# Four node stages of a graph network: the normalized rows made by ScalarE instead of VectorE

## The reference: what is computed

```python
def _layernorm(x, axis=-1, eps=1e-05):
    m = jnp.mean(x, axis=axis, keepdims=True)
    v = jnp.var(x, axis=axis, keepdims=True)
    return (x - m) / jnp.sqrt(v + eps)
...
x = _layernorm(x + _L0_gnn_ref(x, edge_weight, src, dst, ...))
x = _layernorm(x + _L1_gnn_ref(x, L1_gnn_factors, src, dst, ...))
x = _layernorm(x + _L2_gnn_ref(x, edge_index, L2_gnn_W, L2_gnn_a_l, L2_gnn_a_r))
x = _layernorm(x + _L3_gnn_ref(x, L3_gnn_W_in, L3_gnn_W_out, src, dst))
```

## Time and profile before

| | |
|---|---|
| median of 3 runs | 5793.68 us (5790.52 to 5794.18) |
| the profiled execution: its own time | 5795.6 us |
| its span from first to last instruction | 5793.8 us |
| busy share of the span: PE, DVE, ACT, POOL | 59%, 42%, 24%, 63% |
| mean granted TensorE clock | 0.735 of full speed |

### The profile page before, as it was taken

How to read it: one execution, slowest core, us unless ns; L and a number is a source line. 1 busy time by engine, 2 the same in 40 slices (tenths; PEclk the granted TensorE clock), 3 DMA queues, 4 the chain that set the end, 5 groups by cost and what they waited for, 6 DMA issues and landing times. The chain is left out here.

```text
span 5793.8 us, 95902 instructions
## 1 busy us (share of the span) xinstructions
PE 3447.0 (59%) x19621; PEld 2711.1 (47%) x19621; DVE 2417.4 (42%) x3906; ACT 1387.4 (24%) x3059; POOL 3658.6 (63%) x3808
## 2 busy tenths in 40 slices
PE   1258988889669998466666662333333443333335
PEld 0246565556458886466656561333333333333333
DVE  3323333333546666366666664222222222222224
ACT  0012222222224443133333231111111211111111
POOL 2267777777611013777777774777777767777776
PEclk9779999999889999588888885555555565555557
DMA  9969999999479997466666653455544444444443
GB/s 231 306 183 291 298 300 301 304 298 296 124 234 332 327 331 231 138 182 181 181 181 186 177 168 87 131 131 131 131 131 131 124 114 131 131 131 131 131 131 106
DMA packets 809797, 1127.80 MB, mean 195 GB/s; under 512 B 128769, under 2 KB 490874, under 8 KB 806362
## 3 DMA queue, kind: packets, MB, share of 16 engines
q1 hardware_dynamic: 368424, 431.55, 24.3%
q0 software_dynamic: 134688, 305.12, 21.5%
q10 hardware_dynamic: 306588, 390.09, 20.2%
HBM read 688.68 MB, written 438.07 MB: 194 GB/s over the span
## 5 line engine op out<-in xcount | busy, mean ns | idle before, releaser
L1114 POOL DMA_INDIRECT gath<-sender_table,idx x1664 | 1570.2, 944 | 577.0 <-issue 413.5
L1318 DVE TENSOR_TENSOR_SCAN scan<-meta,scan,bank 128x512 f32<-128x512 bf16 x624 | 798.6, 1280 | 1943.2 <-DVEq L1315 1942.8
L1187 PE MATMUL bank<-ident,gath 128*128 128x128 f32 x1664 | 464.1, 434 | 1277.5 <-DMA gath<-sender_table,idx 1277.5
L1114 POOL DMA_INDIRECT gath<-joint_table,idx x832 | 810.4, 974 | 298.9 <-issue 208.2
L1507 POOL DMA_INDIRECT gath<-attention_table,idx x832 | 814.1, 978 | 263.3 <-issue 191.7
L1187 PEld LDWEIGHTS bank<-ident,gath 128*128 128x128 f32 x1664 | 297.8, 217 | 1443.5 <-DMA gath<-sender_table,idx 1443.5
L1255 ACT ACTIVATE rows<-bank 128x512 f32<-128x512 f32 x624 | 372.6, 597 | 1149.9 <-ACTq L1253 1121.5
L738 POOL DMA_INDIRECT gath<-scan_rows,end_i x196 | 188.9, 964 | 646.2 <-ACTq L1432 574.7
L1213 PE MATMUL bank<-ident,scan 128*128 128x128 f32 x2496 | 568.6, 373 | 4.5 <-PEq L1211 4.5
L1213 PEld LDWEIGHTS bank<-ident,scan 128*128 128x128 f32 x2496 | 470.6, 202 | 130.5 <-issue 130.5
L1194 PE MATMUL bank<-ident,gath 128*128 128x128 f32 x1664 | 372.5, 309 | 0.0
(11 more groups left out here) (239 smaller groups left out, 5569.5 us busy)
## 6 DMA issues: line engine op xcount, KB each, us to landing
recv<-receiver_rows SPq DMA_DIRECT2D x624, 256.0 KB
scan_rows<-rows ACTq DMA_DIRECT2D x624, 256.0 KB
attention_scan_rows<-rows ACTq DMA_DIRECT2D x208, 264.0 KB
receiver_rows<-gath ACTq DMA_DIRECT2D x26, 2048.0 KB, 12.1
meta<-edge_meta SPq DMA_DIRECT2D x208, 256.0 KB
factor_rows<-gath ACTq DMA_DIRECT2D x208, 256.0 KB
meta<-edge_meta SPq DMA_DIRECT2D x416, 128.0 KB
gath<-factor_rows SPq DMA_DIRECT2D x208, 256.0 KB
```

The source lines that it names most:

```text
L1114: pool.indirect_dma_start(out=landed[s][:, c, 0:width], out_offset=None, in_=table[:, :], in_offset=bass.IndirectOffsetOnAxis(ap=idx[s][:, ...
L1187: ins = pe.transpose(b[:, c * P:(c + 1) * P], g[:, c, 0:F], ident[:, :])
L1318: chain(v.tensor_tensor_scan(scan[s % 2][:, :], go_on, src, scan[1 - s % 2][:, EB - 1:EB], ALU.add if k == 1 else ALU.mult, ALU.max if k = ...
```

## The change

DVE no longer writes the normalized rows. Its piece `normalize` becomes `scale`, with two small instructions per group: the reciprocal of the deviation (as before) and shift = -mean x reciprocal. ACT gets a piece `normalize` of the same lag, placed behind `turned_x` and ahead of `deviation`: for each tile an ACTIVATE of the function Identity with the reciprocal as its scale and the shift as its bias, one number per partition each. `rstd` has two buffers now, and `shift` too. Three semaphores are new: `n_scale` (DVE to ACT, once per group), `n_scale_free` and `n_y_free` (ACT to DVE: the scale's and `y_nm`'s buffers may be written again, two groups later).

```diff
-        stats = sb("stats", [P, CT, 6]); mv = [sb(f"mv{s}", [P, CT, 2]) for s in range(2)]; std = [sb(f"std{s}", [P, CT]) for s in range(2)]; rstd = sb("rstd", [P, CT])
+        stats = sb("stats", [P, CT, 6]); mv = [sb(f"mv{s}", [P, CT, 2]) for s in range(2)]; std = [sb(f"std{s}", [P, CT]) for s in range(2)]; rstd = [sb(f"rstd{s}", [P, CT]) for s in range(2)]; shift = [sb(f"shift{s}", [P, CT]) for s in range(2)]
...
+        n_scale = sem("n_scale"); n_scale_free = sem("n_scale_free"); n_y_free = sem("n_y_free")
...
 def update(q, s):
...
+                    if norm and q > 0:
+                        v.wait_ge(n_y_free, 1)
+                        v.sem_inc(n_y_free, -1)
...
-                def normalize(q, s):
+                def scale(q, s):
                     w = GROUP_TILES[2 * q + s]
-                    x, y = x_nm[:, tiles(q, s), :], y_nm[s][:, 0:w, :]
                     v.wait_ge(n_std, 1)
                     v.sem_inc(n_std, -1)
-                    chain(v.reciprocal(rstd[:, 0:w], std[s][:, 0:w]))
-                    for c in range(w):
-                        v.tensor_scalar(x[:, c, :], y[:, c, :], mv[s][:, c, 0:1], rstd[:, c:c + 1], ALU.subtract, ALU.mult).then_inc(v_done, 1)
-                    v.wait_ge(v_done, w)
-                    v.sem_inc(v_done, -w)
-                    if turn:
-                        v.sem_inc(n_x, 1)
-                    if k in (3, 5):
-                        v.sem_inc(n_tab, 1)
+                    if q > 0:
+                        v.wait_ge(n_scale_free, 1)
+                        v.sem_inc(n_scale_free, -1)
+                    chain(v.reciprocal(rstd[s][:, 0:w], std[s][:, 0:w]))
+                    v.scalar_tensor_tensor(shift[s][:, 0:w], mv[s][:, 0:w, 0], -1.0, rstd[s][:, 0:w], ALU.mult, ALU.mult).then_inc(n_scale, 1)
...
-                work = [(new + 3, receivers)] * makes_recv + [(new + 3, add_c2)] * (k == 0) + [(late + 1, normalize)] * norm + [(late, update), (0, aggregate)] * gathers
+                work = [(new + 3, receivers)] * makes_recv + [(new + 3, add_c2)] * (k == 0) + [(late + 1, scale)] * norm + [(late, update), (0, aggregate)] * gathers
...
 def scalar(act):
...
+                def normalize(q, s):
+                    w = GROUP_TILES[2 * q + s]
+                    act.wait_ge(n_scale, 1)
+                    act.sem_inc(n_scale, -1)
+                    for c in range(w):
+                        act.activation(x_nm[:, (2 * q + s) * CT + c, :], y_nm[s][:, c, :], ACT.Identity, scale=rstd[s][:, c:c + 1], bias=shift[s][:, c:c + 1]).then_inc(a_done, 1)
+                    act.wait_ge(a_done, w)
+                    act.sem_inc(a_done, -w)
+                    if 2 * q + s + 2 < NG:
+                        act.sem_inc(n_scale_free, 1)
+                        act.sem_inc(n_y_free, 1)
+                    if turn:
+                        act.sem_inc(n_x, 1)
+                    if k in (3, 5):
+                        act.sem_inc(n_tab, 1)
...
-                work = ([(new + 2, table)] * (w_tab is not None) + [(new + 1, turned_x)] * turn + [(late, deviation)] * norm
+                work = ([(new + 2, table)] * (w_tab is not None) + [(new + 1, turned_x)] * turn + [(late + 1, normalize), (late, deviation)] * norm
                         + [(1, hidden), (0, keep_aggT)] * dense)
```

## The result

The changed kernel is **slower by 1.1%**: 5854.87 us median of 4 runs (5851.33 to 5859.28), the kernel before 5792.1 us beside it (4 runs, 5789.15 to 5794.18), ratio 1.0109 with a 95% interval of 1.0092 to 1.0127. The forecast was 5775.7 us, with a range of 5768 to 5784: wrong in size and in sign.

What follows compares the result with a forecast made beforehand. POOL was taken to bound stage 1, DVE's round 7 stage 2, DVE's chain stage 3, gathers then DVE's drain stage 5. 5793.7 - (0 + 0.5 + 12.8 + 4.7 = 18.0) = 5775.7 us, range 5768 to 5784.

Steps and rivals of the forecast that it cites:

- All the rest of the span: Everything outside the four changed stages, some 5390 us: no changed instructions, so taken to keep its length.
- a sum of -18.0: Whole kernel: 0 from stage 1, 0.5 from stage 2, 12.8 from stage 3 and 4.7 us from stage 5, all earlier.
- The last line of the forecast: The forecast falls if L999 takes over 0.6 us or the untouched sweeps between the stages change their length.
- its one rival for a slower kernel: Stage 3: four ACTIVATEs over 4.9 us (1.2 us each) lengthen ACT's round; at 1.5 us each about 5810 us; 4%.
- Stage 1: POOL's back-to-back chain of indirect DMAs sets the end and hides the change: 0 us.
- The rival in which POOL is helped: Stages 1 and 2: without L897 blocking POOL's DMAs, they end 3 and some 2 us earlier, 5770.5 us; 10%.
- Stage 2: First scatter 0.5 us earlier, since ACT's four instructions delay the square root; ends 3.7 us earlier and 1 us later.
- Stage 3: DVE's chain: twelve groups save 1.22 us each, 14.65 us, less 1.8 at the end: 12.8 us earlier.
- the sum had 1.7: ACT's price per group: four ACTIVATEs of 0.42 us without overlap make 1.7 us.
- Stage 5: Gathers keep their pace, DVE's drain shortens: 0.3 + 2.8 + 2.4 - 0.8 = 4.7 us earlier.
- the bounds of the DVE price: DVE's saving per full group: 0.94 us if new waits cost 0.33 us, 1.45 us if the small instruction hides wholly.
- the rivals for the stages: ACT slower, about 5779 us (12%); time given back in waits, about 5791 (8%); slower (4%); POOL helped, 5770.5 (10%).

Runs made afterwards that it cites:

- the changed kernel with 38 on DVE: Changed kernel plus 38 do-nothing instructions at the end of DVE's stage 2 program, against the kernel before: 7597.53 us, ratio 1.0093.
- the one with 88 on DVE: Kernel before plus 88 do-nothing instructions at the end of DVE's stage 2 program, against the kernel before without them: 5856.06 us, ratio 1.0095.

## Why the prediction was wrong

**The step that failed** is a sentence of its first paragraph: "All the rest of the span, some 5390 us, has none of the changed instructions." That is true, and from it I let the rest keep its length: a term of nothing, with no reason but that its instructions are the same. The edit changes the length of two engines' programs ahead of every later loop. What the runs show in its place is +73.0 us in the attention sweep, against a sum of -18.0. The last line of the forecast named a sweep that changes its length as what would bring it down, but no rival had a mechanism for it, and its one rival for a slower kernel, at 4%, was ACT's pace in stage 3. A listing of the program with the count of instructions ahead of each loop would have told that a loop of 263 instructions moves by 220 places and can touch three blocks or four; it would not have told which, for by the count alone the loop would be at place 67 and touch three.

The section Instruction fetch mechanics of the page "Runtime: NRT & Kernel Launch" of the Trainium skill has the rule that I did not weigh: fetching is purely sequential, and "a taken branch whose target isn't in the current 2-page window forces a DMA fetch of the target page before execution can continue". The trace agrees in kind, with 2.4 us at the jump. In size it does not: the page speaks of 16 KiB pages, and queue 14 moved 8192 bytes at a time. The two differ in one run. With pages of 256 instructions DVE's 307 would lie in two of them in the changed kernel with 38 on DVE (place 91), and would stay loaded; but DVE's jump took 3.6 to 4.6 us there in all ten turns, and 90 packets came between ACT's jumps, where ACT alone makes 45. It does not hang on the 60: with pages of 256, of which two stay, no number in its place lets both this run and the one with 88 on DVE load again, since their loops lie 130 places apart and only the last 50 places of a page reach into a third. Blocks of 128 explain all fourteen rows; the page's figure of 32 KiB in all, four blocks, would make room for three and the one that is fetched ahead. That this is why four don't fit is argued, not shown.

**Stage 1: 0, forecast 0.** First gather to first scatter 46.1 us (46.0), to the last scatter 126.0 (125.9; the earlier trace rows):

```profile
L748 POOL DMA_INDIRECT receiver_rows<-same,start_i x49: 983/985/1496, 1519.4 to 1599.3; - x49
```

The rival in which POOL is helped falls: POOL was busy for 104.11 us instead of 104.00, with DVE's L897 gone.

**Stage 2: 0 at the first scatter, forecast 0.5.** The square root stands behind ACT's four instructions as drawn, and DVE's gain goes into the wait for it. POOL waits for 26.23 us as before:

```profile
2250.43 1.65 ACT L999 ACTIVATE x_nm<-recv,shift,rstd 128x128 f32<-128x128 f32 x4 [0.35 <-ACTq L997]
2252.51 0.30 ACT L991 ACTIVATE std<-mv,eps 128x4 f32<-128x4 f32 x1 [0.43 <-ACTq L990]
```

```profile
2259.26 1.02 POOL L748 DMA_INDIRECT receiver_rows<-same,start_i  x1 [26.23 <-POOLq L745]
```

**Stage 3: -12.1, forecast -12.8.** The updates come 4.87 us apart instead of 6.10, so a group saves 1.23 us (forecast 1.22). From the first to the last update it is 58.4 us instead of 73.2, 14.8 (14.65). The end gave back 2.7 us, not 1.8. The lines of the update and of the two new instructions (durations min/median/max in ns; L999 and L904 over all stages):

```profile
L877 DVE TENSOR_TENSOR recv<-x_nm,recv x13: 293/693/693, 3542.9 to 3601.3; 128x512 f32<-128x512 f32 x12, 128x128 f32<-128x128 f32 x1
```

```profile
L999 ACT ACTIVATE x_nm<-recv,shift,rstd x196: 477/480/497, 1498.3 to 5846.0; 128x128 f32<-128x128 f32 x196
```

```profile
L904 DVE SCALAR_TENSOR_TENSOR shift<-mv,rstd x52: 159/162/222, 1497.3 to 5845.7; 128x4 f32<-128x4 f32 x48, 128x1 f32<-128x1 f32 x4
```

One L999 takes 0.48 us, not 0.42, but four overlap to 1.65 us, where the sum had 1.7 and the estimate from the Trainium skill (page "ScalarE: Activation LUTs") 1.64. L904 takes 0.16 us; the nearest row had been 0.18.

**Stage 5: -4.0, forecast -4.7.** From L904 to the last L999 0.29 us pass, and the square root of the last tile waits for group 11, as drawn:

```profile
5842.92 1.65 ACT L999 ACTIVATE x_nm<-recv,shift,rstd 128x128 f32<-128x128 f32 x4 [0.87 <-ACTq L997]
...
5844.86 0.29 ACT L991 ACTIVATE std<-mv,eps 128x1 f32<-128x1 f32 x1 [0.30 <-ACTq L990]
...
5845.72 0.16 DVE L904 SCALAR_TENSOR_TENSOR shift<-mv,rstd 128x1 f32<-128x1 f32 x1
...
5846.01 0.49 ACT L999 ACTIVATE x_nm<-recv,shift,rstd 128x128 f32<-128x128 f32 x1 [0.86 <-ACTq L997]
```

So the stages gave some 16 of the 18 us. What is missing is 0.7 us in stage 3 (its end), 0.5 in stage 2 and 0.7 in stage 5. (The range had a slip too: the bounds of the DVE price come to 3.7 us faster and 4.5 slower, where it has -4.2 and +3.9.) The kernels in which ACT's loop does not move into a fourth block are faster by 0.33%: on the faster chip ratios of 0.9967, where the forecast's is 0.9969. On one of the slower chips it was 0.9956 and 0.9966; on the other nothing could be told from noise. Of the rivals for the stages none came.

**Where the 73 us lie.** The stops at the jump and behind it make 52 of them. Told by ACT's writes of rows, the pause with the stop in it takes 21.7 to 22.3 us instead of 16.1, which is 54 us in nine turns; the seven blocks behind it take 25.7 to 27.7 us instead of 24.9, 16 us in all; the other pause of the turn 16.3 to 16.8 instead of 16.1, 4 us. The seven blocks go with TensorE's granted clock. In its 14 us behind the stop it is 0.76 in five of the turns, with 25.7 to 26.1 us for the seven blocks, and 0.58 to 0.60 in the other four, with 27.6 or 27.7. Behind the pauses of the kernel before, from 2798 us on, it is 0.91 to 0.93, with 24.6 to 24.9 us, and the one time that it was 0.75 behind the same pause as the stop's (at 2673.9) they took 26.2 us there as well. The view of windows for two of these turns, changed:

```profile
3032.70:3046.70 14.00, 8.85 (x42) 8.88 (x43) 8.13 (x12) 5.17 (x14) 8.12 (x9) 0.58 0.52 150
3124.40:3138.40 14.00, 8.13 (x53) 8.00 (x54) 8.16 (x12) 5.79 (x15) 8.10 (x9) 0.76 0.51 152
```

and behind a pause of the kernel before:

```profile
3043.80:3057.80 14.00, 12.39 (x98) 11.91 (x97) 10.68 (x17) 6.02 (x16) 10.74 (x11) 0.91 0.69 195
```

The kernel before has its stretch at 1.2 GHz (0.5) from 3032.6 to 3046.2, most of it inside the pause, which ends at 3043.8. In the changed kernel one such stretch ends at 3028.2, TensorE has its wait of 6.72 us until 3037.85, and the next stretch lies from 3035.0 to 3048.7, on the first blocks behind the stop. That the clock makes these blocks longer fits every turn, but no run sets it apart.

**What stays open.** Why a fourth block isn't kept. And the two stalls together cost no more than one on the chip where they were tried.

## What to carry to other kernels

An edit in straight code moves every loop behind it on the same engine. For each long loop count how many blocks of 128 instructions it touches before and after; here three was free and four cost 65 to 91 us in a sweep of ten turns. The count alone is not the place: here 60 had to be added, and it was known only from the trace of a kernel that loads, so take every loop that can touch one block more as one that may. Look at the code queue of the page (66 packets, then 114): if it grows by some packets for every turn of a loop, it is the first suspect. Fix the loop's place where the language can, and judge the edit only then: here the same edit is +1.1% or -0.33%.

## What I had not expected of the hardware

- A loop of 263 instructions that had run without a single load was loaded again in each of nine turns, 5 packets of 8192 bytes a turn, when its code moved by 220 instructions.
- The boundary of a block is to be seen in the trace: the first instruction of the loop ran 2.4 us after the jump and the second 4.0 us after the first, each behind a load of its own (3026.9 and 3030.9). So the first is the last of its block, place 127. 1987 instructions ahead make place 67 by the count, so the code lies 60 places further than counted; that six more instructions move the head into the next block fits.
- DVE pays in another form than ACT: 3.6 to 5.0 us at the jump alone, with the head in the middle of a block (place 93) and the fourth block at the loop's end.
